# Token scalings as one GpSimd product per tile, and a norm-factor chain of two GpSimd operations

## The chip, the cores and the metric

The kernel runs on one core of a Trainium2 chip. The metric is the device time of one execution in microseconds (us). TensorE does the matrix products, VectorE, ScalarE and GpSimd the elementwise work; in the profile they are PE (with PEld for its weight loads), DVE, ACT and POOL. Each engine takes its instructions in the order in which they were written, and engines wait for each other through semaphores (`wait_ge`, `then_inc`).

## What is computed

One transformer layer of width 256 on 2048 tokens (32 sequences of 64): attention with quantized projections, then a mixture of experts (the second part is not touched). Cut to what matters here:

```
def _div_clamp_fp8(x, scale):
    y = jnp.clip(x / scale, -448, 448)
    return _fp8_roundtrip(y.astype(bfloat16).astype(float32))
ln_out = _ln(hidden_states, ln_w, ln_b)
q  = _ln(linear(_div_clamp_fp8(ln_out, q_in_scale),  wq),  qln_w,  qln_b)
k  = _ln(linear(_div_clamp_fp8(ln_out, k_in_scale),  wk),  kln_w,  kln_b)
v  =     linear(_div_clamp_fp8(ln_out, v_in_scale),  wv)
qx = _ln(linear(_div_clamp_fp8(ln_out, qx_in_scale), wqx), qxln_w, qxln_b)
kx = _ln(cond @ w_kx, kxln_w, kxln_b);  vx = cond @ w_vx
out = linear(_div_clamp_fp8(concat(attend(q, k, v), attend(qx, kx, vx)), smooth), wproj)
```

So every token tile is divided by four different vectors (K, Q, V and QX), clipped and rounded to fp8 values: four quantized copies. `_ln` over a head of 128 needs, for each token and head, a factor (variance + 1e-5)^(-1/2).

## The kernel before

The tokens are NT = 16 tiles of 128. Attention over them is 64 slots, four to a tile (r = 0 to 3): r is the half of the heads, with self attention in r = 0, 1 and cross attention in r = 2, 3. In a slot N the engines work on several slots at once, as a software pipeline: `run_slots` goes through a written list of steps for each engine, each with a number "ahead", and calls the step for slot N + ahead. Nothing is planned at run time: the lists are the order of the instructions.

In a slot PE does four projections into `b_pj` (L346) for slot N+3, three groups of transposes of normalised heads (L362, `b_tr<-ident,nrm`) for N+2, the scores (L374), the transposes of the probabilities (L393), the products with the values (L403) and the output projection (L446). ACT squares each projection (L458, `sq`), copies it (L468, `raw`), and evicts transposes (L485, with the weight and bias of the head norm from `col`). DVE sums the squares (L526, `ssq`), and multiplies `raw` by the norm factor (L537, `nrm<-raw,rstd`) before PE transposes it; it also does the softmax (L546 to L569), `cat` (L578) and `catq` (L587, L593), the quantizing of attention's output.

Two steps are touched by the change.

The norm factors (`pool_rstd`, L693 to L704) are on POOL: four operations from `ssq` to `rstd`, var = ssq * unit2, vareps = var + eps, root = vareps^(-1/2), rstd = root * unit. They run twice in a slot: once on 4 factors (the K heads, for `nrm` 0 of that slot) and once on 8 (the Q heads, for `nrm` 1 and 2 at the start of the next).

The token scalings belong to the steps with "ahead" PREP = 7: a tile's tokens are prepared seven slots early, in parts 0 to 3. In part 0 DVE normalises (L671, `n<-x_sb`), PE transposes (L628), ACT evicts with the layer norm's weight and bias (L637, `lnT`). In each of the four parts ACT then divides `lnT` by one of the four scales (L647, `y<-lnT,rin`, two instructions, one for each half of the width), and DVE clips (L678, `xq<-y`) and rounds (L682, `xq<-xq`) that copy. On POOL stands besides, once in a tile, a small layer norm for the second half of the kernel (`pool_rows`, L716 to L720, `zero<-x_sb`: names are those of the memory, its result is called n3).

Of the kernel before, what the change touches and what calls it, by code (L numbers as in the profile page):

```python
# [5 lines left out]
F32 = mybir.dt.float32  # L6
F16 = mybir.dt.float16
BF16 = mybir.dt.bfloat16
# [57 lines left out]
def build(nc, x, ctxT, cols, w_all, wprojT,  # L66
# [4 lines left out]
    with ExitStack() as top:  # L71
# [6 lines left out]
        def sem(name):  # L78
# [51 lines left out]
                 "small_done st_done t_done ssum_done stot_done sstep sinv_done wsq4_done csum_done ctot_done wscale_done n2_done tr_done ctx_step "  # L130
                 "ctxh_done xh_done lnt_done raw_done proj_done norm_done tev_done sub_done sc_done pn_done "
                 "ptev_done pt_done cev_done pv_done catq_done x1_done po_done ssq_done sq_done exp_done rs_done "
                 "mx_done sum_done rc_done clip_done pool_var pool_ve pool_pw ve3 rs3 rw_in zero_set xbuf_zero "
# [24 lines left out]
        with ExitStack() as ph:  # L158
# [5 lines left out]
            y16 = sb("y16", [P, 2, KT, P], BF16, ph)  # L164
# [22 lines left out]
            var = sb("var", [P, 2, NN, HC], F32, ph)  # L187
            vareps = sb("vareps", [P, 2, NN, HC], F32, ph)
            root = sb("root", [P, 2, NN, HC], F32, ph)
# [78 lines left out]

            def wide(ap, n):
                return ap.unsqueeze(2).to_broadcast([P, ap.shape[1], n])  # L270
# [50 lines left out]
            def pe_project(c):  # L321
                def step(pe, N):
# [12 lines left out]
                    if r == 0 and c in (0, 1, 3):  # L335
                        pe.wait_ge(s["xq_done"], 4 * i + (1, 2, 0, 3)[c])
                    if r == 2 and c == 1:
                        pe.wait_ge(s["xq_done"], 4 * i + 4)
                    if i == 0:
                        pe.wait_ge(s["wlo_done"], unit_number(r, c, KT - 1) + 1)  # L340
# [135 lines left out]
            def act_tev(c):  # L476
                def step(act, N):
# [6 lines left out]
                    at = C_HLN + 2 * ((HLN_K if c == 0 else HLN_Q) + kind)  # L484
                    act.activation(flat(dst), b_tr[:, :], ACT.Identity, scale=col[:, at:at + 1],  # L485
                                   bias=col[:, at + 1:at + 2]).then_inc(s["tev_done"], 1)
# [144 lines left out]
            def act_token(act, t, part):  # L631
# [3 lines left out]
                after(act, "y_done", 4 * t)  # L635
# [5 lines left out]
            def act_token_scaled(act, t, part):  # L641
# [3 lines left out]
                after(act, "q16_done", 4 * t + part - 1)  # L645
                for k in range(KT):
                    last = act.activation(y16[:, part % 2, k, :], lnT[:, k, :], ACT.Copy, scale=rin[:, j, k:k + 1])  # L647
                last.then_inc(s["y_done"], 1)

# [24 lines left out]
            def dve_quantize(dve, t, part):  # L674
                M = 4 * t + part
                dst = xq_all[:, ring(t), :, PARTS[part], :]
                dve.wait_ge(s["y_done"], M + 1)
                dve.tensor_scalar(dst, y16[:, part % 2, :, :], FP8_MAX * DOWN, -FP8_MAX * DOWN, ALU.min, ALU.max)\  # L678
# [5 lines left out]
            def pool_rstd(q):  # L684
                def step(pool, N):
# [7 lines left out]
                    pool.tensor_tensor(var[:, r % 2, c, :], ssq[:, r % 2, c, :],  # L693
                                       unit2[:, j:j + 1].unsqueeze(2).to_broadcast(shape), ALU.mult)\
                        .then_inc(s["pool_var"], 1)
                    pool.wait_ge(s["pool_var"], e)
# [5 lines left out]
                    pool.wait_ge(s["pool_pw"], e)  # L702
# [89 lines left out]
            def attention_scalar(act, tail):  # L792
# [28 lines left out]
                def context_high(n):  # L821
# [27 lines left out]
                    (PREP, act_token_scaled, "tokens"),  # L849
# [6 lines left out]
                    (-3, "tokens"): lambda: (act_token_scaled(act, 0, 3), act_token(act, 1, 0), act_token_scaled(act, 1, 0)),  # L856
# [1052 lines left out]
```

## Time and profile before

| | before |
|---|---|
| median of 3 runs | 955.73 us (955.66 to 956.96) |
| the profiled execution, its own time | 956.31 us |
| its span, first to last instruction | 954.5 us |
| PE busy | 916.9 us, 96% |
| DVE busy | 793.8 us, 83% |
| ACT busy | 735.6 us, 77% |
| POOL busy | 454.5 us, 48% |

The span has three parts: up to about 110 us the weights and the context are prepared beside the first slots; up to about 635 us the slots run in a pattern that repeats with each tile; then comes the mixture of experts. A matmul's duration in a row includes its way through the array, so that the rows of consecutive matmuls overlap; what a matmul costs is the distance to the start of the next one, and a wait of PE shows as a start that comes later than that. A row with several instructions (x4) begins with the first of them.

### The profile page before, as it was taken

To read this page: it belongs to the slowest core of one execution; us is meant where nothing else is said; L and a number is where in the kernel's file an instruction comes from. 1 tells how busy PE (TensorE), PEld (TensorE's weight loads), DVE (VectorE), ACT (ScalarE), POOL (GpSimd) and SP (SyncE) were. 2 spreads that over 40 slices of the span, in tenths; PEclk is the share of its full clock that TensorE was granted. 3 is DMA by queue.
4 is the path that set the end of the run, shared out by engine and by line. 5 is a ranking of instruction groups with operands and counts; after the bars stand their busy time and mean duration, and the time that the engine had idled before them with its cause. 6 is when DMAs were issued, how large, how long until landed. Compare 5 with 4: busy or idle time off the path is not lost.

```text
span 954.5 us, 23599 instructions
## 1 busy us (share of the span) xinstructions
PE 916.9 (96%) x8264; PEld 621.1 (65%) x8264; DVE 793.8 (83%) x1720; ACT 735.6 (77%) x1370; POOL 454.5 (48%) x673
## 2 busy tenths in 40 slices
PE   5688999999999999999999999999999999999997
PEld 3365666766767676766767667666655566666665
DVE  6889999999999999999999999987998744444443
ACT  5998899899899899899999999864656545555554
POOL 5335656465565555555555555531056513333333
PEclk9989999999999999999999999999999999999999
DMA  9933201001001001001100100213558713333323
GB/s 215 333 90 70 64 24 51 30 30 44 29 30 46 29 29 46 29 30 31 44 30 24 52 29 24 102 44 117 178 157 262 249 48 54 51 74 51 46 32 37
DMA packets 36754, 70.48 MB, mean 74 GB/s; under 512 B 3616, under 2 KB 24736, under 8 KB 36512
## 3 DMA queue, kind: packets, MB, share of 16 engines
q1 hardware_dynamic: 27184, 54.39, 17.5%
q0 software_dynamic: 9456, 14.59, 9.1%
q8 instruction: 70, 1.15, 0.5%
q14 instruction: 44, 0.36, 0.1%
HBM read 55.52 MB, written 18.68 MB: 78 GB/s over the span
## 4 chain that ended last, share of the span: by engine, by line
PE 64%; DVE 21%; issue 7%; ACT 5%; POOL 1%; DMA 1%; DVEq 0%; POOLq 0%; ACTq 0%
PE b_pj L346 17%; PE b_tr L362 7%; PE b_pj L1339 5%; PE b_o L403 5%; PE b_o L1374 5%; PE b_sc L374 4%; PE b_acc L446 4%; PE b_o L1466 3%; PE b_tr L1339 3%; DVE ssq L526 3%; PE b_sc L1339 3%; DVE nrm L537 3%; PE b_pj L1419 2%; DVE cat L578 2%; PE b_pt L1363 2%
## 5 line engine op out<-in xcount | busy, mean ns | idle before, releaser
L700 POOL TENSOR_TENSOR root<-vareps,neghalf 128x4 f32<-128x4 f32 (+1 forms) x128 | 173.8, 1358 | 10.0
L693 POOL TENSOR_TENSOR var<-ssq,unit 128x4 f32<-128x4 f32 (+1 forms) x128 | 54.3, 424 | 235.1 <-DVE ssq L526 235.1
L346 PE MATMUL b_pj<-w_hi,xq 128*128 128x512 f16 x384 | 148.9, 388 | 1.1 <-DVE xq L682 0.8
L346 PE MATMUL b_pj<-w_lo,xq 128*128 128x512 f16 x384 | 148.3, 386 | 0.0
L526 DVE TENSOR_REDUCE ssq<-sq 128x4 f32<-128x512 f32 x192 | 130.3, 679 | 3.3 <-ACT sq L458 2.1
L537 DVE TENSOR_TENSOR nrm<-raw,rstd 128x512 f32<-128x512 f32 x192 | 128.8, 671 | 4.2 <-POOL rstd L704 3.5
L362 PE MATMUL b_tr<-ident,nrm 128*128 128x128 f32 x768 | 120.5, 280 | 11.6 <-DVE nrm L537 7.0
L458 ACT ACTIVATE sq<-b_pj 128x512 f32<-128x512 f32 x192 | 114.2, 595 | 18.2 <-PE b_pj L346 14.7
L1315 POOL DMA_INDIRECT out<-xn x39 | 60.6, 1553 | 136.2 <-ACT xn L1545 110.5
L362 PEld LDWEIGHTS b_tr<-ident,nrm 128*128 128x128 f32 x768 | 87.7, 141 | 48.3 <-DVE nrm L537 18.1
L468 ACT ACTIVATE raw<-b_pj 128x512 f32<-128x512 f32 x192 | 116.0, 604 | 0.0
L485 ACT ACTIVATE qT<-b_tr,col 128x512 f32<-128x512 f32 x128 | 99.7, 779 | 1.4 <-PE b_tr L362 1.4
L578 DVE TENSOR_TENSOR cat<-b_o,rsm 128x512 bf16<-128x512 f32 x128 | 81.9, 682 | 1.4 <-PE b_o L403 1.4
L374 PEld LDWEIGHTS b_sc<-kT,qT 128*64 128x64 f32 x2048 | 64.9, 138 | 18.6 <-issue 14.6
L374 PE MATMUL b_sc<-kT,qT 128*64 128x64 f32 x2048 | 73.8, 225 | 0.7 <-ACT qT L485 0.7
L403 PE MATMUL b_o<-probT,v 64*128 64x128 f32 x1024 | 74.4, 285 | 0.0
L403 PEld LDWEIGHTS b_o<-probT,v 64*128 64x128 f32 x1024 | 62.1, 188 | 11.5 <-issue 11.5
L446 PE MATMUL b_acc<-wproj,catq 128*128 128x256 f16 x512 | 66.4, 273 | 0.0
L346 PEld LDWEIGHTS b_pj<-w_hi,xq 128*128 128x128 f16 x384 | 37.8, 99 | 33.1 <-issue 1.4
L492 ACT ACTIVATE prob<-prob 128x512 f32<-128x512 f32 x64 | 40.7, 636 | 22.4 <-DVE prob L553 22.1
L485 ACT ACTIVATE kT<-b_tr,col 128x512 f32<-128x512 f32 x64 | 49.5, 774 | 9.6 <-PE b_tr L362 8.4
L346 PEld LDWEIGHTS b_pj<-w_lo,xq 128*128 128x128 f16 x384 | 38.1, 99 | 25.2 <-issue 1.9
(327 smaller groups left out, 2271.7 us busy)
## 6 DMA issues: line engine op xcount, KB each, us to landing
nst<-in_ffw SPq DMA_DIRECT2D x40, 512.0 KB, 3.3
wload<-in_ffw SPq DMA_DIRECT2D x20, 512.0 KB, 4.5
xbuf<-zero SPq DMA_DIRECT2D x13, 387.0 KB, 9.6
xn<-xbuf SPq DMA_DIRECT2D x9, 516.0 KB, 3.7
x_sb<-in_x SPq DMA_DIRECT2D x4, 512.0 KB, 14.1
wproj<-in_ctxT SPq DMA_DIRECT2D x1, 2048.0 KB, 10.9
xhl<-in_w_all SPq DMA_DIRECT2D x4, 512.0 KB, 18.2
wproj<-in_wprojT POOLq DMA_DIRECT2D x4, 512.0 KB, 5.0
```

Source lines behind the costliest of these rows:

```text
L346: last = pe.matmul(o, x, w[kind][:, k, at:at + BANK], start=(k == 0 and n_ == 0), stop=(k == KT - 1 and n_ == len(terms) - 1))
L362: last = pe.transpose(o, nrm[:, c, hd * P:(hd + 1) * P], ident[:, :])
L374: last = pe.matmul(b_sc[rows, (g * 2 + b) * S:(g * 2 + b + 1) * S], qT[:, r % 2, g * 2 + b, rows], kT[:, r % 2, g, b * S:(b + 1) * S], sta ...
L403: last = pe.matmul(b_o[b][:, g * P:(g + 1) * P], v[b * S:(b + 1) * S, N % 4, g, :], probT[b * S:(b + 1) * S, r % 2, g, :], start=True, sto ...
L446: last = pe.matmul(out_sum(i), catq[:, r % 2, hd, :], wproj[:, r * n + hd, :], start=(r == 0 and hd == 0 and i != 1), stop=(r == 3 and hd ...
L458: act.activation(sq[:, m % 2, :], b_pj[c % 2][:, :], ACT.Square).then_inc(s["sq_done"], 1)
L468: act.activation(raw[:, r % 2, c, :], bk, ACT.Copy).then_inc(s["raw_done"], 1)
L485: act.activation(flat(dst), b_tr[:, :], ACT.Identity, scale=col[:, at:at + 1], bias=col[:, at + 1:at + 2]).then_inc(s["tev_done"], 1)
L526: dve.tensor_reduce(ssq[:, r % 2, c, :], sq[:, m % 2, :].rearrange("p (a b) -> p a b", b=D), axis=AX.X, op=ALU.add).then_inc(s["ssq_done"], 1)
L537: dve.tensor_tensor(nrm[:, c, :].rearrange("p (a b) -> p a b", b=D), raw[:, r % 2, c, :].rearrange("p (a b) -> p a b", b=D), wide(rstd[:, ...
L700: pool.tensor_tensor(root[:, r % 2, c, :], vareps[:, r % 2, c, :], neghalf[:, 0:1].unsqueeze(2).to_broadcast(shape), ALU.pow).then_inc(s[" ...
L1339: last = pe.matmul(o[:, :], xx[n][:, k * P:(k + 1) * P], w[:, bass.ds(e, 1), at:at + F].rearrange("p a b -> p (a b)"), start=(k == 0 and m ...
```

## The change

The diff, cut to its core (waits, lists and names that follow from it are left out):

```diff
-            y16 = sb("y16", [P, 2, KT, P], BF16, ph)
+            y16 = sb("y16", [P, KT, 4, P], BF16, ph)
+            hw = sb("hw", [P, 4], F32, ph)
...
+            def scaled(t):
+                return 4 * t if t < 2 else t + 6
...
-                    if r == 0 and c in (0, 1, 3):
+                    if i < 2 and r == 0 and c in (0, 1, 3):
...
+                    if i >= 2 and r == 0 and c == 0:
+                        pe.wait_ge(s["xq_done"], scaled(i) + 1)
...
+                    if c == 0 and N in (0, SLOTS.index((0, 2))):
+                        act.wait_ge(s["hw_done"], 1 + kind)
-                    act.activation(flat(dst), b_tr[:, :], ACT.Identity, scale=col[:, at:at + 1],
+                    act.activation(flat(dst), b_tr[:, :], ACT.Identity, scale=hw[:, j:j + 1],
...
+            def pool_token_scaled(pool, t, part):
+                if part != 1:
+                    return
+                pool.wait_ge(s["lnt_done"], KT * t + KT)
+                pool.wait_ge(s["q16_done"], scaled(t))
+                pool.tensor_tensor(y16[:, :, :, :], lnT[:, :, :].unsqueeze(2).to_broadcast([P, KT, 4, P]),
+                                   rin[:, :, :].rearrange("p j k -> p k j").unsqueeze(3).to_broadcast([P, KT, 4, P]),
+                                   ALU.mult).then_inc(s["y_done"], 1)
...
             def dve_quantize(dve, t, part):
-                M = 4 * t + part
-                dst = xq_all[:, ring(t), :, PARTS[part], :]
+                if t >= 2 and part != 2:
+                    return
+                j = slice(0, 4) if t >= 2 else PARTS[part]
+                M = scaled(t) if t >= 2 else 4 * t + part
+                dst = xq_all[:, ring(t), :, j, :]
...
-                    pool.tensor_tensor(var[:, r % 2, c, :], ssq[:, r % 2, c, :],
-                                       unit2[:, j:j + 1].unsqueeze(2).to_broadcast(shape), ALU.mult)\
...
-                    pool.tensor_tensor(vareps[:, r % 2, c, :], var[:, r % 2, c, :],
-                                       epsc[:, 0:1].unsqueeze(2).to_broadcast(shape), ALU.add).then_inc(s["pool_ve"], 1)
+                    pool.tensor_scalar(vareps[:, r % 2, c, :], ssq[:, r % 2, c, :], unit2[:, j:j + 1], EPS,
+                                       ALU.mult, ALU.add).then_inc(s["pool_ve"], 1)
...
-                    pool.tensor_tensor(root[:, r % 2, c, :], vareps[:, r % 2, c, :],
-                                       neghalf[:, 0:1].unsqueeze(2).to_broadcast(shape), ALU.pow).then_inc(s["pool_pw"], 1)
...
-                    pool.tensor_tensor(rstd[:, r % 2, c, :], root[:, r % 2, c, :],
-                                       unit[:, j:j + 1].unsqueeze(2).to_broadcast(shape), ALU.mult)\
+                    pool.tensor_tensor(rstd[:, r % 2, c, :], vareps[:, r % 2, c, :],
+                                       neghalf[:, 0:1].unsqueeze(2).to_broadcast(shape), ALU.pow)\
...
-                    (PREP, act_token_scaled, "tokens"),
...
+                dve.tensor_tensor(hw[:, 0:3], col[:, C_HLN:C_HLN + 6:2], unit[:, 0:3], ALU.mult).then_inc(s["hw_done"], 1)
...
+                    dve.tensor_tensor(hw[:, 3:4], col[:, C_HLN + 6:C_HLN + 7], unit[:, 4:5], ALU.mult).then_inc(s["hw_done"], 1)
...
-                run_slots(pool, [(3, pool_rstd(0)), (3, pool_rstd(1)), (ROWS, pool_rows)],
+                run_slots(pool, [(3, pool_rstd(0)), (3, pool_rstd(1)), (ROWS, pool_rows), (PREP, pool_token_scaled)],
```

For the tiles from 2 on, the four scaled copies are written by one POOL product of 1024 elements in each partition (`y<-lnT,rin`), in part 1, instead of by eight ACT instructions; DVE clips and rounds all four at once, in part 2, instead of one in each part. Tiles 0 and 1 keep the old way. The four POOL operations of a norm factor become two; the factor `unit` is multiplied once, at the start, into the head norm's weight (`hw`), with which ACT evicts the transposes anyway.

The order on POOL in the slot of part 1, before (the chain of the 8 factors, then those of the next slot):

```order
L693 TENSOR_TENSOR var<-ssq,unit 128x8
L697 TENSOR_TENSOR vareps<-var,epsc 128x8
L700 TENSOR_TENSOR root<-vareps,neghalf 128x8
L704 TENSOR_TENSOR rstd<-root,unit 128x8
L693 TENSOR_TENSOR var<-ssq,unit 128x4
L697 TENSOR_TENSOR vareps<-var,epsc 128x4
L700 TENSOR_TENSOR root<-vareps,neghalf 128x4
L704 TENSOR_TENSOR rstd<-root,unit 128x4
```

The same place after the change (POOL):

```order
L712 TENSOR_SCALAR vareps<-ssq,unit 128x8
L716 TENSOR_TENSOR rstd<-vareps,neghalf 128x8
L662 TENSOR_TENSOR y<-lnT,rin 128x1024
L712 TENSOR_SCALAR vareps<-ssq,unit 128x4
L716 TENSOR_TENSOR rstd<-vareps,neghalf 128x4
```

The product stands between the factors of the Q heads of one slot and those of the K heads of the next.

The end of the slot of part 2 and the start of the next on DVE, before:

```order
L587 TENSOR_SCALAR catq<-cat 128x1024
L593 TENSOR_SCALAR catq<-catq 128x1024
L678 TENSOR_SCALAR xq<-y 128x2x128
L682 TENSOR_SCALAR xq<-xq 128x2x128
L546 TENSOR_REDUCE mx<-b_sc 128x8
L537 TENSOR_TENSOR nrm<-raw,rstd 128x512
```

And after (DVE, the same place):

```order
L594 TENSOR_SCALAR catq<-cat 128x1024
L600 TENSOR_SCALAR catq<-catq 128x1024
L697 TENSOR_SCALAR xq<-y 128x1024
L701 TENSOR_SCALAR xq<-xq 128x1024
L553 TENSOR_REDUCE mx<-b_sc 128x8
L544 TENSOR_TENSOR nrm<-raw,rstd 128x512
```

The pair stays in the list in this slot and is four times as large; in the slots of parts 0, 1 and 3 nothing stands in its place.

## Rows read from the trace of the kernel before

**Rows 1.** Busy time (and instructions) by engine in one tile's stretch, then clock, DMA:

```profile
294.70:331.30 36.60, 36.52 (x373) 25.60 (x372) 35.39 (x73) 33.43 (x65) 20.82 (x36) 1.00 0.10 34
```

**Rows 2.** Timeline of PE: start, duration, line, operands, count:

```profile
305.81 0.38 PE L346 MATMUL b_pj<-w_lo,xq 128*128 128x512 f16 x1
306.27 0.66 PE L362 MATMUL b_tr<-ident,nrm 128*128 128x128 f32 x4
...
324.73 0.38 PE L346 MATMUL b_pj<-w_lo,xq 128*128 128x512 f16 x1
324.95 0.60 PE L362 MATMUL b_tr<-ident,nrm 128*128 128x128 f32 x4
```

**Rows 3.** Waits of PE, 75 to 112 us: total, times, longest:

```profile
PE b_tr L362 <- DVE nrm L537: 3.9, 5, 1.3
```

**Rows 4.** Waits of PE's weight loads, 330 to 367 us:

```profile
PEld b_tr L362 <- DVE nrm L537: 0.6, 1, 0.6
```

**Rows 5.** Waits of PE, 587 to 625 us:

```profile
PE b_tr L362 <- DVE nrm L537: 1.0, 1, 1.0
```

**Rows 6.** Chain of waits through one tile: start, length, what:

```profile
330.84 0.69 ACT y L647 x2
...
342.84 0.66 PE b_tr L362 x4
```

**Rows 7.** Timeline of DVE in the same tile, with idle time before and its releaser:

```profile
301.78 0.64 DVE L537 TENSOR_TENSOR nrm<-raw,rstd 128x512 f32<-128x512 f32 x1
302.34 0.69 DVE L569 TENSOR_TENSOR prob<-prob,rc 128x512 f32<-128x512 f32 x1
...
306.73 0.69 DVE L537 TENSOR_TENSOR nrm<-raw,rstd 128x512 f32<-128x512 f32 x1
...
312.18 0.42 DVE L587 TENSOR_SCALAR catq<-cat 128x1024 f16<-128x1024 bf16 x1
312.63 0.43 DVE L593 TENSOR_SCALAR catq<-catq 128x1024 uint16<-128x1024 uint16 x1
312.97 0.22 DVE L678 TENSOR_SCALAR xq<-y 128x256 f16<-128x256 bf16 x1
313.23 0.23 DVE L682 TENSOR_SCALAR xq<-xq 128x256 uint16<-128x256 uint16 x1
313.37 0.42 DVE L618 SCALAR_TENSOR_TENSOR xr<-zero,xr 128x256 f16<-128x256 f32 x1
...
314.40 0.69 DVE L537 TENSOR_TENSOR nrm<-raw,rstd 128x512 f32<-128x512 f32 x1
...
319.89 0.64 DVE L537 TENSOR_TENSOR nrm<-raw,rstd 128x512 f32<-128x512 f32 x1
...
323.28 0.69 DVE L537 TENSOR_TENSOR nrm<-raw,rstd 128x512 f32<-128x512 f32 x1 [0.23 <-POOL rstd L704]
...
331.55 0.23 DVE L678 TENSOR_SCALAR xq<-y 128x256 f16<-128x256 bf16 x1 [0.52 <-ACT y L647]
```

**Rows 8.** Timeline of POOL in the same tile:

```profile
301.84 0.65 POOL L693 TENSOR_TENSOR var<-ssq,unit 128x8 f32<-128x8 f32 x1 [1.13 <-DVE ssq L526]
302.56 0.52 POOL L697 TENSOR_TENSOR vareps<-var,epsc 128x8 f32<-128x8 f32 x1
303.17 1.69 POOL L700 TENSOR_TENSOR root<-vareps,neghalf 128x8 f32<-128x8 f32 x1
304.94 0.20 POOL L704 TENSOR_TENSOR rstd<-root,unit 128x8 f32<-128x8 f32 x1
...
306.11 1.23 POOL L720 TENSOR_SCALAR zero<-x_sb,mv,rs 128x256 f32<-128x256 f32 x1
...
308.65 1.03 POOL L700 TENSOR_TENSOR root<-vareps,neghalf 128x4 f32<-128x4 f32 x1
```

**Rows 9.** Other POOL operations, grouped by line and shape: busy, mean ns:

```profile
L1107 POOL MEMSET zero<- 128x1548 f16 x1 | 1.4, 1407 | 0.0
L1091 POOL TENSOR_SCALAR_AFFINE_SELECT ident<-ident 128x128 f32<-128x128 f32 x1 | 0.3, 291 | 0.3 <-POOL ident L1089 0.3
```

More of the change, by code:

```diff
@@ L334, in step @@
                         terms = ((j, w_hi), (j, w_lo))
-                    if r == 0 and c in (0, 1, 3):
+                    if i < 2 and r == 0 and c in (0, 1, 3):
                         pe.wait_ge(s["xq_done"], 4 * i + (1, 2, 0, 3)[c])
-                    if r == 2 and c == 1:
+                    if i < 2 and r == 2 and c == 1:
                         pe.wait_ge(s["xq_done"], 4 * i + 4)
+                    if i >= 2 and r == 0 and c == 0:
+                        pe.wait_ge(s["xq_done"], scaled(i) + 1)
                     if i == 0:
@@ L483, in step @@
                     dst = kT[:, r % 2, :, :] if c == 0 else qT[:, r % 2, (c - 1) * 4:c * 4, :]
-                    at = C_HLN + 2 * ((HLN_K if c == 0 else HLN_Q) + kind)
-                    act.activation(flat(dst), b_tr[:, :], ACT.Identity, scale=col[:, at:at + 1],
-                                   bias=col[:, at + 1:at + 2]).then_inc(s["tev_done"], 1)
+                    if c == 0 and N in (0, SLOTS.index((0, 2))):
+                        act.wait_ge(s["hw_done"], 1 + kind)
+                    j = (HLN_K if c == 0 else HLN_Q) + kind
+                    at = C_HLN + 2 * j + 1
+                    act.activation(flat(dst), b_tr[:, :], ACT.Identity, scale=hw[:, j:j + 1],
+                                   bias=col[:, at:at + 1]).then_inc(s["tev_done"], 1)
                 return step
@@ L634, in act_token @@
                 act.wait_ge(s["tr_done"], t + 1)
-                after(act, "y_done", 4 * t)
+                after(act, "y_done", scaled(t))
                 for k in range(KT):
@@ L644, in act_token_scaled @@
                     act.wait_ge(s["lnt_done"], KT * t + KT)
-                after(act, "q16_done", 4 * t + part - 1)
+                after(act, "q16_done", 4 * t + part - 3)
                 for k in range(KT):
-                    last = act.activation(y16[:, part % 2, k, :], lnT[:, k, :], ACT.Copy, scale=rin[:, j, k:k + 1])
+                    last = act.activation(y16[:, k, j, :], lnT[:, k, :], ACT.Copy, scale=rin[:, j, k:k + 1])
                 last.then_inc(s["y_done"], 1)
+            def pool_token_scaled(pool, t, part):
[6 more added lines that the diff above has]
+                                   ALU.mult).then_inc(s["y_done"], 1)
             def dve_scale_chain(dve, n, at, sums):
@@ L674, in dve_quantize @@
             def dve_quantize(dve, t, part):
-                M = 4 * t + part
-                dst = xq_all[:, ring(t), :, PARTS[part], :]
+                if t >= 2 and part != 2:
[3 more added lines that the diff above has]
+                dst = xq_all[:, ring(t), :, j, :]
                 dve.wait_ge(s["y_done"], M + 1)
-                dve.tensor_scalar(dst, y16[:, part % 2, :, :], FP8_MAX * DOWN, -FP8_MAX * DOWN, ALU.min, ALU.max)\
+                dve.tensor_scalar(dst, y16[:, :, j, :], FP8_MAX * DOWN, -FP8_MAX * DOWN, ALU.min, ALU.max)\
                     .then_inc(s["q16_done"], 1)
@@ L860, in attention_scalar @@
                     (-2, "raw 3"): lambda: high(2, 4),
-                    (-2, "token"): lambda: (high(2, 5), squares(0)),
-                    (-2, "tokens"): lambda: (squares(1), high(3, 2), squares(2)),
+                    (-2, "token"): lambda: (high(2, 5), squares(0), squares(1), high(3, 2), squares(2)),
                     (-2, "rows"): lambda: (high(3, 3), squares(3)),
@@ L868, in attention_scalar @@
                     (-1, "raw 2"): lambda: act_token_scaled(act, 1, 3),
-                    (-1, "tokens"): lambda: (high(2, 0), high(2, 1)),
+                    (-1, "token"): lambda: (high(2, 0), high(2, 1)),
                     (0, "weight squares"): lambda: high(2, 6),
@@ L1586, in shared @@
                     return run
-                tail = {(FIRST - 3, "tokens"): shared(0), (FIRST - 2, "raw 1"): shared(1), (FIRST - 1, "raw 3"): units_known}
+                tail = {(FIRST - 3, "token"): shared(0), (FIRST - 2, "raw 1"): shared(1), (FIRST - 1, "raw 3"): units_known}
                 for n in range(JOIN):
@@ L1592, in _ @@
                 for n in range(2, 6):
-                    tail[FIRST - 2 + n, "tokens"] = shared(n)
+                    tail[FIRST - 2 + n, "token"] = shared(n)
                 attention_scalar(act, tail)
```

11 lines of the change are left out of this document (3 added, 8 removed).

## The prediction

> **What bounds the kernel now.** I read the busy times by stretch first, then PE's timeline and its waits, then the chain of waits, then DVE and POOL beside each other in one tile. In a tile of the repeating part PE is busy 36.52 of 36.60 us, DVE 35.39, ACT 33.43, POOL 20.82, with the clock at its higher level of 2.4 GHz (granted 1.00) [rows 1]. A busy PE may still hide waits, so the starts decide. Where nothing is late, the transposes of `nrm` start 0.22 us after the start of the last projection matmul (324.73 to 324.95); at 305.81 the same pair is 0.46 us apart [rows 2]. PE thus waits 0.24 to 0.25 us, for `nrm` from DVE. I went along all starts of PE: this wait comes once in a tile, from 196 to 562 us in eleven tiles, and once as 0.46 us in the tile before. The list of waits has it as the single wait for `nrm` in a tile (0.6 us on the weight loads, which run ahead of the matmuls) [rows 4]. So from 110 to 600 us PE is the bound, and all that the other engines can give back is about 3.2 us. The rest lies at the ends: 3.9 us of waits for `nrm` in five places between 75 and 112 us, where DVE also prepares the context [rows 3], and 1.0 us near 599 us [rows 5].
>
> The chain shows why `nrm` is late: it leaves PE for ACT's scaling `y` of part 3 at 330.84, goes on over DVE, and comes back to PE's transposes at 342.84 [rows 6]. 342.84 less 306.27 [rows 2] is the period of a tile, 36.57 us. DVE had stood idle for 0.52 us for that `y` [rows 7].
>
> **The change, part by part.**
>
> ACT's eight scalings in a tile go, 0.69 us for a pair [rows 6]. ACT is not the bound; what counts is that DVE no longer waits for them: 0.52 us in part 3.
>
> On DVE, a clip and a rounding of one copy take 313.37 - 312.97 = 0.40 us from start to start; the same two on 1024 elements, the pair that quantizes attention, take 312.97 - 312.18 = 0.79 us [rows 7]. The change removes 0.40 in parts 0, 1 and 3 and adds 0.39 in part 2: 0.81 us less in a tile, 1.33 with the wait. In part 2's slot `nrm` ends at 323.28 + 0.69 = 323.97, and PE takes it at 324.95 [rows 2, 7]: 0.98 us of cover for the added 0.39. In the slots of parts 3 and 0, which lead to the late `nrm`, DVE gains 0.92 and 0.40 us, and 0.25 is wanted.
>
> On POOL, the 8 factors take from 301.84 to 305.14. `var` is 0.65 us long beside an `nrm` on DVE and ends 0.07 after it; `vareps` is 0.52 beside `prob`, and ends 0.05 after that [rows 7, 8]; without such a neighbour an operation of this size takes the 0.20 of `rstd`. POOL thus stands still while DVE reads two SBUF tensors. In the new chain the first operation still waits for `nrm`, and the power then waits for `prob` in place of `vareps`, so only `rstd` and its gap go and a little of the power's delay: about 0.35 us of 3.3. The factors of the K heads gain two small operations with their gaps, 0.55 us. `nrm` was 0.23 us late by POOL in one slot of a tile [rows 7]; that place moves with DVE, and nothing replaces it.
>
> The product is new: 1024 elements from two f32 operands. The trace has no POOL operation like it, so bounds: a MEMSET writes 1548 elements in 1.41 us, which makes 0.93 us for 1024; the AFFINE_SELECT reads and writes 128 in 0.29, 2.3 us for 1024 [rows 9]; n3 takes 1.23 for 256, 4.9 us for 1024 [rows 8]. I take 2.4 us, by the AFFINE_SELECT, the row nearest in kind, and keep 0.9 and 4.9 for the range. It starts right after the 8 factors, at about 314.05 (`nrm` at 314.40 marks their end today, less 0.35) [rows 7]. Two `nrm` lie in its way, which hold POOL for 0.6 us each: it ends at 314.05 + 2.4 + 1.2 = 317.65. Behind it the K factors need 0.20 + 0.07 + 1.03 = 1.30 [rows 8] and are there at 318.95; the `nrm` that takes them starts at 319.89, or 0.4 earlier now [rows 7]. So it is hidden, with 0.5 us to spare. The quantizing that waits for it stands nine microseconds later.
>
> The Trainium skill (GPSIMD Engine Reference, 3.1 Elementwise) gives a two-input `tensor_tensor` of 2048 elements 4497 ns on GpSimd. An estimate from that page is 2.25 us for the product; by it the sum stays the same, and no row here shows it.
>
> `hw` adds two tiny DVE operations at the start, 0.1 us on the way; the eviction reads another scale, at the same price.
>
> The sum: twelve repeated waits, 11 x 0.25 + 0.46 = 3.2 us. Of the 3.9 us early on, DVE has 0.40 less in parts 0 and 1 of tile 2 and a shorter POOL chain, against 0.39 more in part 2: I take 1.0. Of the 1.0 near 599 us, where part 3 of the last tile stands a slot ahead, 0.3. After 600 us 0.2 from the shorter chain. Less 0.1 for `hw`: 4.6 us. The profiled execution's 956.31 becomes 951.7; it was 0.58 above the median of the runs, 955.73, which becomes 951.1.
>
> **Rivals.**
>
> DVE held by the product (22%). `nrm` and the product read SBUF at the same time. Suppose that POOL, once it has begun, keeps DVE's two-tensor operations off until its end. `nrm` 1 goes first, the product begins behind it, and `nrm` 2, due 0.6 us later, is held for 2.4 - 0.6 = 1.8 us. DVE carries this into part 2's slot with 0.39 more and 0.40 less, against the cover of 0.98: PE waits 0.8 us in each of 14 tiles, 11.2 us less the 4.6: 962.3. Should `nrm` 1 be held as well, nothing covers it: up to 2.4 x 14 = 34 us. Against it: n3 runs from 306.11 to 307.34, and the `nrm` that starts within it, at 306.73, lasts 0.69 us as always [rows 7, 8]; likewise at all its sixteen places. For it: n3 is short and may have read all before. The Trainium skill (SBUF — State Buffer, SBUF: two separate sides) states exactly this rival: whichever starts first has the shared pair for its whole instruction, and the other is fully blocked. For `var` behind `nrm` the trace agrees; for `nrm` within n3 it doesn't.
>
> The product is long (8%). It decides above 319.49 - 1.30 - 1.2 - 314.05 = 2.9 us. At n3's 4.9, the K factors come 2.0 us late, DVE stands for it and 0.39 more follows: against the cover of 0.98, PE waits about 1.0 us in 14 tiles, less 4.6: 965.
>
> The gain doesn't arrive (13%). PE has no slack of its own, and `nrm` may be late behind something else, for instance ACT's squares, which set when `ssq` can start. Then only the early part gives something: 955.0.
>
> **How the numbers follow.** Forecast 57%: 951.1, its own range 948.5 (all waits of rows 3 and 5 gone as well) to 953.5. Of the rest, 30% is slower and 13% mostly no change. What a measurement of this kernel can tell from no change is 0.2%, 1.9 us. Faster: the forecast's 57% and a little of the third rival, 0.59; same 0.13; slower 0.28. The range is 948.5 to 962.5: it takes in the first rival's lower price and the third, and leaves out the long product and a `nrm` 1 that is held.
>
> **What would show it.** PE's start of the transposes 0.22 us behind the projection in every slot, and a period of 36.3 us for a tile. POOL's product at 2.3 to 3.6 us, the K factors done before `nrm` asks. DVE without a wait for `y`, and in part 1's slot `nrm` 1 and 2 still 1.2 us apart. Wrong it is when these two move apart by more than a microsecond, when a wait of `nrm` for `rstd` grows in the slot of part 2, or when the period stays 36.57.

## The result, and the profile after

The changed kernel takes 964.6 us (963.49 to 967.39, 4 runs), against 955.72 (955.66 to 956.96, 4 runs) for the kernel before on the same chip: 1.0095 times as long, with an interval of 1.0082 to 1.0107. It is slower by 8.9 us; forecast was 951.1, and the range ended at 962.5. One run of e10 (968.86 us) and one of e11 (1060.55 us) fell into a slower state of the chip, and all medians below are of the other, fast runs. The profiled run is the longest of the four, 967.39 us with a span of 965.6.

The first two rows of the page of the changed kernel show the load where it was meant to be: ACT and POOL have less to do.

```profile
span 965.6 us, 23136 instructions
...
PE 917.1 (95%) x8264; PEld 621.5 (64%) x8264; DVE 807.9 (84%) x1638; ACT 704.2 (73%) x1258; POOL 446.2 (46%) x431
```

ACT has lost 31 us and PE has the same work. But DVE, which was to be relieved of 0.81 us in every tile, is busy 14 us longer. The groups by line name the one that grew: `nrm` on DVE, and next to it POOL's new product (busy time and mean ns of one, then idle time before).

```profile
L544 DVE TENSOR_TENSOR nrm<-raw,rstd 128x512 f32<-128x512 f32 x192 | 150.5, 784 | 3.7 <-POOL rstd L716 0.9 <-issue 0.2
...
L366 PE MATMUL b_tr<-ident,nrm 128*128 128x128 f32 x768 | 120.8, 280 | 18.2 <-DVE nrm L544 14.4 <-ACT kT L492 1.9 <-ACT qT L492 1.8
...
L662 POOL TENSOR_TENSOR y<-lnT,rin 128x1024 bf16<-128x1024 f32 x14 | 26.6, 1897 | 0.0
```

The same 192 `nrm` were 128.8 us busy before, 671 ns each: 21.7 us have come in. A mean of 784 hides that nearly all of them are unchanged. The busy times of one tile give the place to look at: a stretch of one period, to hold against [rows 1].

```profile
300.53:337.53 37.00, 36.50 (x372) 25.58 (x370) 36.38 (x69) 31.04 (x58) 20.58 (x20) 1.00 0.10 33
```

A tile now takes 37.00 us where it took 36.58 (the distance from an `nrm` to the same one ten tiles later, divided by ten, in each of the two traces). PE's busy time hardly moved and its clock is the same granted 1.00; DVE is at 36.38 of 37.00. The timeline of DVE around the product, with start and duration (the counterpart of [rows 7]), shows why:

```profile
316.23 0.69 DVE L553 TENSOR_REDUCE mx<-b_sc 128x8 f32<-128x512 f32 x1
317.04 2.38 DVE L544 TENSOR_TENSOR nrm<-raw,rstd 128x512 f32<-128x512 f32 x1
319.35 0.68 DVE L560 TENSOR_TENSOR prob<-b_sc,mx 128x512 f32<-128x512 f32 x1
319.95 0.68 DVE L544 TENSOR_TENSOR nrm<-raw,rstd 128x512 f32<-128x512 f32 x1
```

And the timeline of POOL at the same place (that of [rows 8]):

```profile
314.00 1.23 POOL L712 TENSOR_SCALAR vareps<-ssq,unit 128x8 f32<-128x8 f32 x1 [1.60 <-DVE ssq L533]
315.32 1.69 POOL L716 TENSOR_TENSOR rstd<-vareps,neghalf 128x8 f32<-128x8 f32 x1
316.98 1.90 POOL L662 TENSOR_TENSOR y<-lnT,rin 128x1024 bf16<-128x1024 f32 x1
321.32 0.27 POOL L712 TENSOR_SCALAR vareps<-ssq,unit 128x4 f32<-128x4 f32 x1 [2.44 <-DVE ssq L533]
```

Both things wait for the power at L716. When it ends, POOL goes on in its own list and starts the product at 316.98; DVE is released by the same end, and starts `nrm` 1 at 317.04, 0.06 us later. That `nrm` lasts 2.38 us instead of 0.68. It ends at 319.42, which is 0.54 after the product's end at 318.88: about the length of an undisturbed `nrm`. So it did nothing while the product ran. PE's timeline has the price:

```profile
318.60 0.38 PE L350 MATMUL b_pj<-w_lo,xq 128*128 128x512 f16 x1
319.48 0.66 PE L366 MATMUL b_tr<-ident,nrm 128*128 128x128 f32 x4 [0.50 <-DVE nrm L544]
...
321.82 0.38 PE L350 MATMUL b_pj<-w_lo,xq 128*128 128x512 f16 x1
322.03 0.60 PE L366 MATMUL b_tr<-ident,nrm 128*128 128x128 f32 x4
...
346.56 0.38 PE L350 MATMUL b_pj<-w_lo,xq 128*128 128x512 f16 x1
346.78 0.60 PE L366 MATMUL b_tr<-ident,nrm 128*128 128x128 f32 x4
```

PE could have started at 318.60 + 0.22 = 318.82 and started at 319.48, 0.66 late. `nrm` 1 undisturbed would have ended at 317.72, with 1.10 us to spare for PE; it was held for 2.38 - 0.68 = 1.70; 1.70 - 1.10 is 0.60, and 0.06 is the step from the end of the one to the start of the other. At the two other places PE runs 0.21 and 0.22 us behind the projection, and the one at 346.78 answers, counted along PE's instructions, to the late one of the kernel before (306.27 in [rows 2], 342.84 a tile later): the wait of 0.24 that the change was to remove has gone.

One product lies in the early part, beside the preparation of the context, where it hits another DVE operation with two SBUF tensors. From the timelines of POOL and then of DVE:

```profile
91.36 1.89 POOL L662 TENSOR_TENSOR y<-lnT,rin 128x1024 bf16<-128x1024 f32 x1
```

```profile
91.33 3.00 DVE L1012 SCALAR_TENSOR_TENSOR ctxl<-wproj,nsc,ctxh 128x1024 f16<-128x1024 f32 x1
...
103.26 1.28 DVE L1012 SCALAR_TENSOR_TENSOR ctxl<-wproj,nsc,ctxh 128x1024 f16<-128x1024 f32 x1
```

Here DVE's record even begins 0.03 us before the product's, and it is still the one that is stretched, by 1.72 us. PE's transposes behind it waited 1.19 us in place of 0.24.

### The profile page after: what moved, and what is told of

Its sections match the earlier page's. It is cut to its first block, busy times and chain, and to the rows that moved or that the text cites. A ratio compares the mean times of both kernels' runs of the same rounds, so it can differ in the third digit from the quotient of the medians.

```text
span 965.6 us, 23136 instructions
## 1 busy us (share of the span) xinstructions
PE 917.1 (95%) x8264; PEld 621.5 (64%) x8264; DVE 807.9 (84%) x1638; ACT 704.2 (73%) x1258; POOL 446.2 (46%) x431
## 4 chain that ended last, share of the span: by engine, by line
PE 31%; POOL 28%; issue 24%; DVE 12%; ACT 4%; another core or an unknown queue 0%; POOLq 0%; DVEq 0%; ACTq 0%
POOL rstd L716 14%; POOL vareps L712 8%; PE b_o L1386 5%; PE b_pj L1351 5%; PE b_pj L350 3%; PE b_tr L1351 3%; PE b_sc L1351 3%; PE b_o L1478 2%; POOL y L662 2%; PE b_pt L1375 2%; POOL zero L732 2%; PE b_pj L1431 2%; DVE a L1776 1%; PE b_sc L1431 1%; ACT w_hi L813 1%
## 5 line engine op out<-in xcount | busy, mean ns | idle before, releaser
L712 POOL TENSOR_SCALAR vareps<-ssq,unit 128x4 f32<-128x4 f32 (+1 forms) x128 | 93.2, 728 | 266.8 <-DVE ssq L533 266.6
L716 POOL TENSOR_TENSOR rstd<-vareps,neghalf 128x4 f32<-128x4 f32 (+1 forms) x128 | 173.0, 1351 | 10.7
L544 DVE TENSOR_TENSOR nrm<-raw,rstd 128x512 f32<-128x512 f32 x192 | 150.5, 784 | 3.7 <-POOL rstd L716 0.9
L492 ACT ACTIVATE qT<-b_tr,col,hw 128x512 f32<-128x512 f32 x128 | 100.6, 786 | 1.8 <-PE b_tr L366 1.8
L492 ACT ACTIVATE kT<-b_tr,col,hw 128x512 f32<-128x512 f32 x64 | 50.1, 782 | 25.6 <-PE b_tr L366 25.5
```

Of the source, the lines that this page charges most:

```text
L492: act.activation(flat(dst), b_tr[:, :], ACT.Identity, scale=hw[:, j:j + 1], bias=col[:, at:at + 1]).then_inc(s["tev_done"], 1)
L544: dve.tensor_tensor(nrm[:, c, :].rearrange("p (a b) -> p a b", b=D), raw[:, r % 2, c, :].rearrange("p (a b) -> p a b", b=D), wide(rstd[:, ...
L712: pool.tensor_scalar(vareps[:, r % 2, c, :], ssq[:, r % 2, c, :], unit2[:, j:j + 1], EPS, ALU.mult, ALU.add).then_inc(s["pool_ve"], 1)
L716: pool.tensor_tensor(rstd[:, r % 2, c, :], vareps[:, r % 2, c, :], neghalf[:, 0:1].unsqueeze(2).to_broadcast(shape), ALU.pow)\
```

## The experiments

Changes are given against the changed kernel where nothing else is said. "Period" is the time of a tile in the repeating part, measured as above; "at the end of the slots" is how much later (+) than in the trace of the kernel before the instructions around 640 us start. That column is no finer than about 1 us: at 60 us, ahead of every product, the traces of the changed kernel and of e1, e2, e5, e6, e7, e8, e10 and e11 hold the same instructions and already lie between 0.9 us early and 0.2 us late, and the stretches before 58 us in which PE's clock was granted at 0.50 (1.2 GHz) differ among them. The kernel before was run again beside every group of them, with medians of 956.2 to 956.3 us.

| | median us | ratio to before, interval | period | at the end of the slots |
|---|---|---|---|---|
| changed kernel | 964.6 | 1.0095 (1.0082 to 1.0107) | 37.00 | +7.1 |
| e1_wait: product waits for `nrm` 2 | 951.68 | 0.996 (0.9946 to 0.9973) | 36.29 | -4.9 |
| e8_ahead: product first in the list | 951.96 | 0.9958 (0.9942 to 0.9973) | 36.29 | -5.1 |
| e2_no_product | 953.89 | 0.9976 (0.9966 to 0.9986) | 36.29 | -3.8 |
| e4_tokens_only | 967.53 | 1.0119 (1.0104 to 1.0135) | 37.33 | +10.3 |
| e3_chain_only | 956.73 | 1.0003 (0.9994 to 1.0012) | 36.58 | +0.5 |
| e7_twice | 973.79 | 1.0183 (1.016 to 1.0206) | 37.66 | +17.3 |
| e5_split4 | 953.44 | 0.997 (0.9958 to 0.9982) | 36.29 | -3.6 |
| e6_one_input | 952.41 | 0.997 (0.9946 to 0.9994) | 36.29 | -5.2 |
| e9_wait_old_chain | 952.8 | 0.9967 (0.9956 to 0.9978) | 36.28 | -3.9 |
| e10_eight_scalars | 953.03 | 0.9973 (0.9964 to 0.9983) | 36.28 | -4.3 |
| e11_after_first | 954.61 | 0.999 (0.9974 to 1.0006) | 36.28 | -3.1 |

**e1_wait: the product at a place without a neighbour.** Nothing is removed; the product only waits until both `nrm` of the slot are done.

```diff
                 pool.wait_ge(s["q16_done"], scaled(t))
+                pool.wait_ge(s["norm_done"], NN * (4 * t - 3) + NN)
                 pool.tensor_tensor(y16[:, :, :, :], ...
```

> The changed kernel with one wait more: the product waits until nrm 2 of the next slot is done, and so runs beside the sum of squares and cat. Theory (the product keeps DVE's two-tensor nrm from starting for its whole 1.9 us): no nrm over 0.7 us, no wait of PE for nrm in the tile, period 36.3 to 36.4 us instead of 37.0, in all 950 to 953 us. Rival (the loss comes from the other edits: the shorter POOL chain's slower first operation of 1.23 us, or the pair of 1024 elements on DVE): the nrm shortens but the period stays near 37.0 and the time within 960 to 965.

Measured: 951.68 us, the period 36.29. POOL's timeline, then DVE's:

```profile
309.10 1.69 POOL L717 TENSOR_TENSOR rstd<-vareps,neghalf 128x8 f32<-128x8 f32 x1
312.88 1.90 POOL L663 TENSOR_TENSOR y<-lnT,rin 128x1024 bf16<-128x1024 f32 x1 [2.10 <-DVE nrm L544]
314.76 0.27 POOL L713 TENSOR_SCALAR vareps<-ssq,unit 128x4 f32<-128x4 f32 x1
```

```profile
310.82 0.69 DVE L544 TENSOR_TENSOR nrm<-raw,rstd 128x512 f32<-128x512 f32 x1
312.03 0.68 DVE L544 TENSOR_TENSOR nrm<-raw,rstd 128x512 f32<-128x512 f32 x1
316.64 0.64 DVE L544 TENSOR_TENSOR nrm<-raw,rstd 128x512 f32<-128x512 f32 x1
```

The same product with the same length, 2.1 us later, and every `nrm` has its old duration. The factors behind it are ready at 316.13, before the `nrm` that takes them, at 316.64. One line is worth 12.9 us against the changed kernel (964.6 - 951.68), and the result is 0.4% faster than the kernel before, with an interval that leaves out 1. None of DVE's operations beside the product (`ssq`, `sm`, `cat`) reads two large SBUF tensors. The place of the product was the whole loss.

**e8_ahead: the same, with another order on POOL.** The product comes first in POOL's list for the slot and waits for the `nrm` of the slot before.

```diff
+                pool.wait_ge(s["norm_done"], NN * (4 * t - 4) + NN)
...
-                run_slots(pool, [(3, pool_rstd(0)), (3, pool_rstd(1)), (ROWS, pool_rows), (PREP, pool_token_scaled)],
+                run_slots(pool, [(PREP, pool_token_scaled), (3, pool_rstd(0)), (3, pool_rstd(1)), (ROWS, pool_rows)],
```

> The changed kernel with the product first in POOL's list of the slot of part 1 (one slot half earlier than with the wait in the next slot), behind a wait for nrm 2 of the same slot. Theory: no nrm is held, the same gain as with the other wait, 951 to 952.5 us; the ctxl operations at 77 to 104 us lie elsewhere, so the start may differ by 1 us. Rival (POOL is late with the factors of the K heads): nrm 0 waits for rstd in this slot, over 953 us.

Measured: 951.96, with the period of e1. It is not a property of one gap: it is enough that none of DVE's `nrm` is due in the 1.9 us.

**e2_no_product: the product nearly taken out.** One column of 128 is left of it, except in tile 2; the tokens of the later tiles are thus mostly not scaled.

```diff
-                pool.tensor_tensor(y16[:, :, :, :], lnT[:, :, :]...to_broadcast([P, KT, 4, P]),
+                m = P if t == 2 else 1
+                pool.tensor_tensor(y16[:, :, :, 0:m], lnT[:, :, 0:m]...to_broadcast([P, KT, 4, m]),
```

> The changed kernel with the product left out for the tiles from 3 on (one column of 128 is written, so the quantized tokens are wrong there). It is the most that the change can give without the product's cost. Theory: 950 to 953 us, the same as with the wait. Rival (other edits lose): over 958 us.

Measured: 953.89, 0.9 us above the range that I had expected, and far from the rival's 958. The period is 36.29, to the hundredth that of e1 with the whole product. Well placed, the product costs nothing in a tile. The 1.1 us by which it ends later than e1 stem from tile 2, whose product is whole and unmoved here: its instructions around 119 us are 0.4 late, those of e1 0.7 early.

**e4_tokens_only and e3_chain_only: the two halves of the change apart.** e4 is the kernel before with the product and the pair of four scales, and the old chain of four operations; e3 is the kernel before with the new chain and `hw`, and ACT's scalings as they were.

```diff
 e4, against the changed kernel
-                    pool.tensor_scalar(vareps..., ssq..., unit2[:, j:j + 1], EPS, ALU.mult, ALU.add)
+                    pool.tensor_tensor(var..., ssq..., unit2..., ALU.mult)
+                    pool.tensor_tensor(vareps..., var..., epsc..., ALU.add)
...
-                    pool.tensor_tensor(rstd..., vareps..., neghalf..., ALU.pow)
+                    pool.tensor_tensor(root..., vareps..., neghalf..., ALU.pow)
+                    pool.tensor_tensor(rstd..., root..., unit..., ALU.mult)
 e3, against the changed kernel
-                pool.tensor_tensor(y16[:, :, :, :], ...
+                    last = act.activation(y16[:, part % 2, k, :], lnT[:, k, :], ACT.Copy, scale=rin[:, j, k:k + 1])
```

> The kernel before with the product and the merged pair, and the old chain of four POOL operations. Theory: nrm 1 is held as in the changed kernel, DVE is a little later by POOL's longer chain: 963 to 967 us. Rival (the chain is what loses): within 2 us of the kernel before.

> The kernel before with the chain of two POOL operations and the head norm's weight scaled at the start; the tokens as before. Theory: the chain of the 8 factors is 0.3 us shorter, but nrm is late by DVE and not by POOL in the slot that holds PE up, so little changes in the tile: 954 to 955.5 us. Rival (the chain costs): 957 us or more.

Measured: the tokens alone are slower still (967.53), the chain alone makes no difference (956.73; the interval of the ratio takes in 1). They lie 0.5 and 1.2 us above their expected ranges. Of e4, POOL and then DVE:

```profile
318.05 1.91 POOL L661 TENSOR_TENSOR y<-lnT,rin 128x1024 bf16<-128x1024 f32 x1
```

```profile
318.13 2.37 DVE L543 TENSOR_TENSOR nrm<-raw,rstd 128x512 f32<-128x512 f32 x1 [0.41 <-POOL rstd L722]
```

The hold is the same with the old chain. It costs more here, since `nrm` also waits 0.41 us for POOL: PE starts 0.99 late, and the period is 0.33 longer than with both halves. In one tile of e4 the order is the other one: `nrm` 1 starts at 169.49 us, 0.13 ahead of the product. There `nrm` 1 has its usual 0.69 us, the product takes 2.33, `nrm` 2 takes 1.80, and PE doesn't wait for either. So the loss does not come from the chain; and a chain that is 0.3 us shorter is worth nothing by itself, since ACT's `y`, not POOL, ends DVE's wait in that kernel [rows 7].

**e7_twice: twice the suspected cost.** The product is made twice, the first time into memory that nobody reads.

```diff
+                for dst in (y16b, y16):
-                pool.tensor_tensor(y16[:, :, :, :], ...
+                    last = pool.tensor_tensor(dst[:, :, :, :], ...
```

> The changed kernel with the product issued twice, first into a scratch tile and then as before. Theory (the hold is a price on DVE, lasting as long as the product): DVE is held for 1.9 us more, either in nrm 1 or in nrm 2. PE had 0.66 us of wait for the first 1.9 us; the cover is used up, so nearly all of the second comes through: 1.5 to 1.9 us in 14 tiles, 985 to 992 us. Rival (POOL itself is what is late): the factors of the K heads come later and nrm 0 waits for rstd, nrm 1 stays at 2.4 us; under 975 us.

Measured: 973.79, slower by 9.2 than the changed kernel, but well short of the expectation. POOL's timeline, then DVE's:

```profile
321.92 1.90 POOL L664 TENSOR_TENSOR y16b<-lnT,rin 128x1024 bf16<-128x1024 f32 x1
323.77 2.35 POOL L664 TENSOR_TENSOR y<-lnT,rin 128x1024 bf16<-128x1024 f32 x1
```

```profile
321.98 2.38 DVE L545 TENSOR_TENSOR nrm<-raw,rstd 128x512 f32<-128x512 f32 x1
324.89 1.79 DVE L545 TENSOR_TENSOR nrm<-raw,rstd 128x512 f32<-128x512 f32 x1
```

I had let `nrm` 1 be held through both products. It isn't: between the two it gets in, and now the second product is the one that stands, 2.35 - 1.90 = 0.45 us; it then holds `nrm` 2 for 1.79 - 0.68 = 1.11. Per tile PE waits 0.95 and 0.30 us, in place of 0.66. The rival's bound of 975 us holds as well, but not its reason: no `nrm` waits for `rstd` behind the two products. So the hold goes by instruction and in both directions. That pointed to the next experiment.

**e5_split4: the same work in four instructions.**

```diff
+                for j in range(4):
+                    last = pool.tensor_tensor(y16[:, :, j, :], lnT[:, :, :],
+                                              rin[:, j, :].unsqueeze(2).to_broadcast([P, KT, P]), ALU.mult)
```

> The changed kernel with the product as four POOL instructions of 256 elements, one for each scale, at the same place. Theory (the port is held for one instruction and no longer): nrm 1 is held once, by about 0.5 us (a quarter of 1.9), then DVE and POOL take turns; PE's wait of 0.66 us in the tile goes; 951 to 955 us. Rival (a row of POOL instructions keeps DVE out like one): a nrm of 2.4 us or more as now, 963 to 967 us.

Measured: 953.44, at the place where one instruction gave 964.6, without any added wait. POOL (four instructions in a row), then DVE:

```profile
312.05 3.22 POOL L663 TENSOR_TENSOR y<-lnT,rin 128x256 bf16<-128x256 f32 x4
```

```profile
312.12 1.09 DVE L544 TENSOR_TENSOR nrm<-raw,rstd 128x512 f32<-128x512 f32 x1
...
313.73 1.07 DVE L544 TENSOR_TENSOR nrm<-raw,rstd 128x512 f32<-128x512 f32 x1
```

Each `nrm` is held for some 0.4 us, under the 1.10 of cover, and PE doesn't wait for it in the repeating tiles. POOL pays for it: 3.22 us for the four in place of 1.90. They take turns with DVE: the first and third take 0.61 us, the second and fourth, which `nrm` holds in its turn, 1.06.

**e6_one_input: the same writes, one tensor read.** All four copies with the first scale, by an operation whose factor is one number for each partition; the copies thus have the wrong scale, and the eight factors of the second operand are not read.

```diff
-                pool.tensor_tensor(y16[:, :, :, :], lnT..., rin...to_broadcast([P, KT, 4, P]),
+                pool.tensor_scalar(y16[:, :, :, :], lnT..., rin[:, 0, 0:1], None, ALU.mult)
```

> The changed kernel with the product as one POOL TENSOR_SCALAR of 1024 elements: it reads one tensor and multiplies all by a single scale (so the quantized tokens of the tiles from 2 on are wrong there). Theory A (any POOL instruction that reads SBUF holds DVE's two-tensor operations): nrm 1 is as long as this instruction plus 0.5 us, time by its length, 957 to 970 us. Theory B (only a two-tensor instruction of POOL does, which would explain why n3 did not): no nrm over 0.7 us, 951 to 955 us.

POOL, then DVE:

```profile
310.40 3.38 POOL L662 TENSOR_SCALAR y<-lnT,rin 128x1024 bf16<-128x1024 f32 x1
```

```profile
310.45 0.69 DVE L544 TENSOR_TENSOR nrm<-raw,rstd 128x512 f32<-128x512 f32 x1
311.66 0.92 DVE L544 TENSOR_TENSOR nrm<-raw,rstd 128x512 f32<-128x512 f32 x1
```

The operation is 1.8 times as long as the product, started 0.05 us ahead of `nrm` 1 as the product does, and didn't hold it at all; it held `nrm` 2 for 0.24 us. `nrm` 2's 0.92 is 0.22 more than my Theory B allowed. So it isn't the length of the POOL instruction that decides. The kind differs, and with it the second tensor that is read; the run changes both at once. The row of n3 on which I had judged is a TENSOR_SCALAR as well [rows 8].

**e10_eight_scalars: a version of all four scales in that kind.**

```diff
+                for j in range(4):
+                    for k in range(KT):
+                        last = pool.tensor_scalar(y16[:, k, j, :], lnT[:, k, :], rin[:, j, k:k + 1], None, ALU.mult)
```

> The changed kernel with the product as eight POOL TENSOR_SCALARs of 128 elements, each of one tensor and its own scale, at the product's place; it computes the same. In the run with one TENSOR_SCALAR of 1024 elements nrm 1, which began 0.05 us behind it, was not held, and nrm 2 by 0.24 us. Theory (a one-tensor instruction holds DVE for a small part of its time): no nrm over 1.0 us; about 0.6 us each, 4.5 to 5 us for the eight, so the factors of the K heads may come 0 to 1 us late: 951 to 954 us. Rival (each short instruction holds nrm like a part of the product): nrm 1 and 2 over 1.05 us each as with four products, 953 to 955 us.

```profile
311.31 5.39 POOL L664 TENSOR_SCALAR y<-lnT,rin 128x128 bf16<-128x128 f32 x8
```

Measured: 953.03, period 36.28. The eight take 5.39 us, hold `nrm` by 0.1 at most, and are themselves held: the first, begun 0.05 us ahead of `nrm` 1, takes 1.14 us and the third 0.80, where the others take 0.60. They make the later factors late (a later `nrm` waits 0.83 us for POOL), which PE doesn't see. It is as good as e5 and no better than e1.

**e9_wait_old_chain: e4 with the wait of e1.**

> The product behind a wait for nrm 2 of the next slot, with the old chain of four POOL operations (only the tokens are changed). If the gain of the version with the wait comes from DVE's shorter work for the tokens alone, this gives the same within 0.5 us in the repeating part: 951.5 to 952.5 us. If the shorter chain is needed once DVE is earlier (nrm 1 would then wait for rstd), the period lies between 36.28 and 36.57 us: 953 to 955 us.

Measured: 952.8, 0.3 above the first range, but with the period of the first case, 36.28, although `nrm` waits 0.41, 0.23 and 0.34 us for POOL in each tile. The cure thus doesn't need the new chain. Against e1 it is 1.1 us slower by the medians and 0.9 by the traces around 640 us; the intervals of the two ratios overlap, and 0.3 of the 0.9 is there at 60 us, so a gain by the chain is not shown.

**e11_after_first: the order that my first rival had assumed.** The product waits for `nrm` 1 only.

```diff
+                pool.wait_ge(s["norm_done"], NN * (4 * t - 3) + NN - 1)
```

> The changed kernel with a wait of the product for nrm 1 instead of nrm 2: the order that the prediction took for its first rival. Theory (first come, first served, until the end of the instruction): nrm 1 takes 0.69 us, nrm 2 is held and takes 0.68 + 1.9 - 0.6 = about 1.8 to 2.0 us. DVE loses 1.2 us in the tile instead of 1.7; PE needs nrm 2 only 2 us after nrm 1, so less of it comes through: 951.5 to 957 us. Rival (the hold costs the same wherever it falls): 961 us or more.

POOL, DVE and PE:

```profile
313.48 1.90 POOL L663 TENSOR_TENSOR y<-lnT,rin 128x1024 bf16<-128x1024 f32 x1 [0.90 <-DVE nrm L544]
```

```profile
312.61 0.69 DVE L544 TENSOR_TENSOR nrm<-raw,rstd 128x512 f32<-128x512 f32 x1
313.82 2.10 DVE L544 TENSOR_TENSOR nrm<-raw,rstd 128x512 f32<-128x512 f32 x1
```

```profile
316.52 0.38 PE L350 MATMUL b_pj<-w_lo,xq 128*128 128x512 f16 x1
316.73 0.60 PE L366 MATMUL b_tr<-ident,nrm 128*128 128x128 f32 x4
```

`nrm` 2 is held 1.42 us, and PE doesn't wait for it: 316.73 is 0.21 behind the projection, and the period stays 36.28. In this order the hold costs nothing in a tile. Its median is 2.9 us above e1, of which the traces show 1.8 ahead of 640 us, in the early tiles.

## Why the prediction was wrong

**The step that failed** is in the working of the product: "Two `nrm` lie in its way, which hold POOL for 0.6 us each". The holding was there, its direction was wrong. The product does not come behind `nrm` 1: POOL, which takes the next instruction of its own list, started it 0.06 us before DVE, which had to be released, started `nrm` 1. I had computed 314.05 for the start of the product and had 314.40 for that of `nrm` before the change, which is the same 314.05 once the chain's 0.35 is taken off: a tie by my own numbers, since both start at the end of the same POOL operation. I then let `nrm` go first, without a reason, and so put DVE's loss at nothing where 1.70 us were measured. And a two-tensor product that is ahead keeps the `nrm` out to its end. e1, which takes only the coincidence away, moves the time from 964.6 to 951.68. The prediction's own sign of being wrong is there too: `nrm` 1 and 2 start 2.91 us apart, not 1.2.

**The reading that misled.** Against the rival I had put n3, which starts before an `nrm` and doesn't hold it [rows 8]. e6 shows that this says nothing of a product: a TENSOR_SCALAR of 3.38 us holds the first `nrm` by nothing and the next by 0.24, a TENSOR_TENSOR of 1.90 holds it by 1.70. (That `nrm` lies within n3 at 14 of its 16 places, not at all sixteen.) The evidence that the two engines share something was on the same page: `var` and `vareps` on POOL are stretched by DVE's two-tensor operations. Of the reverse case the trace before had only harmless examples, and they were TENSOR_TENSORs. POOL, then DVE, of the kernel before:

```profile
305.45 0.55 POOL L718 TENSOR_TENSOR rs<-ve,neghalf 128x1 f32<-128x1 f32 x1
312.39 1.70 POOL L700 TENSOR_TENSOR root<-vareps,neghalf 128x8 f32<-128x8 f32 x1
```

```profile
305.53 0.68 DVE L537 TENSOR_TENSOR nrm<-raw,rstd 128x512 f32<-128x512 f32 x1
```

Here an `nrm` that starts 0.08 us into `rs` lasts its usual 0.68, and `xr`, which reads two SBUF tensors and starts at 313.37 [rows 7], is not held 0.98 us into a `root` of 1.70 (nor 0.57 into the new chain's power of 1.69). These POOL operations read 1 and 8 elements in each partition, the product 1024. So the kind alone doesn't decide either: a row that clears or accuses the product would have had to be a TENSOR_TENSOR with many elements, and the trace before had none.

The Trainium skill (SBUF — State Buffer, SBUF: two separate sides) states the rule in both directions: of a GpSimd operation and a DVE operation with two SBUF inputs, the first to start has the shared port pair for its whole instruction. For the product the runs agree (2.38, 2.37 and 2.10 us for `nrm`; 3.00 for `ctxl`, though there DVE's record is the earlier by 0.03). For POOL's TENSOR_SCALAR they don't, as e6 and e10 show, nor do they for the short TENSOR_TENSORs above.

**The first rival** (22%) had the mechanism and missed its terms. The order was the other one, `nrm` 1 held and not `nrm` 2. The product took 1.90 us, not 2.4. For a held `nrm` 1 I wrote that "nothing covers it" and put it at up to 34 us; there are 1.10 us of cover, and 0.66 of the 1.70 came through. For a held `nrm` 2 I had 0.8 us of wait in a tile; e11 shows none. That its 962.3 lies 2.3 from the measured time is thus mostly luck. (The lower end of the range was also mis-added: with all waits of [rows 3] and [rows 5] gone it is 947.5, not 948.5. Nothing hangs on it.)

**The sum of the changed kernel**, by its own trace: the repeated 0.25 us waits are gone and 0.66 is new; a tile is 0.42 longer. Against e1 a tile is 0.71 longer, 13 tiles make 9.2. At 119 us, behind tile 2's product, the changed kernel is 2.1 behind e1 (1.4 late against 0.7 early). That is 11.3 of the 12.0 us that lie between the two traces at 640 us. But only 1.5 of the 2.1 come behind the start of that product, where it holds `ctxl`. At 76 us the changed kernel was 0.5 ahead of e1, and at 84 us 0.6 behind, before any product: PE had stood idle for 1.59 us, and then ran with a granted clock of 0.50 (1.2 GHz) up to 83 us, where e1's trace has 1.00. The stretch from 80 us in the trace of the changed kernel (the 0.50 near the end is the clock):

```profile
80.00:81.00 1.00, 1.00 (x5) 0.60 (x4) 1.00 (x3) 0.51 (x3) 0.00 (x0) 0.50 0.00 0
```

No other trace here has the lower clock between 58 us and the last microseconds, so this 1.1 us belongs to the profiled run and not to the change.

**Second rival**, the long product: refuted. It took 1894 to 1901 ns in all 14 places, nearer to the AFFINE_SELECT's 2.3 than to the ends 0.9 and 4.9, and below the 2.9 from which it would matter. e10 shows that even 5.39 us of POOL work at this place costs nothing in a tile: the later `nrm` is 0.83 late by POOL, and PE doesn't see it.

**Third rival**, that the gain doesn't arrive: refuted by e1, where all of it does.

**What was right**, once the product is out of the way: 951.68 us against the forecast 951.1; period 36.29 against 36.3; at the end of the slots 4.9 us early, for a sum of 4.6 (3.3 of it between 160 and 600 us, for 3.2 in the sum; 1.3 from 60 to 160 us, for 1.0; nothing at or behind 600 us, for 0.5); no wait for `y`, and the merged pair, 0.80 us from start to start, hidden. The new chain's gain was about as I had it, for the reason that I gave: its first operation still stands beside `nrm` and `prob` and lasts 1.23 us (0.27 for the four factors, where nothing stands beside it), and from the start of the chain to that of the power it is 315.32 - 314.00 = 1.32 us, before 1.33 [rows 8]. Only `rstd` has gone. e3 and e9 show that this is worth nothing in a tile; ahead of the repeating tiles no gain by it is shown (e3 ends the slots 0.5 us later than the kernel before).

**What stays open.** In its profiled run the changed kernel loses 2.1 us more around 751 us, in the second half of the kernel, where this row stands on DVE (its releaser is not seen), and another 1.7 behind ACT's last instruction:

```profile
751.87 1.41 DVE L1830 SCALAR_TENSOR_TENSOR x_sb<-b_o,us,x_sb 128x512 f32<-128x512 f32 x2 [4.62 <-remote]
```

The change doesn't touch that part, and in e1's trace it runs as before (the same row stands there behind 2.17 us of idle time, for PE). The spans of the other runs of the changed kernel are 963.1, 961.8 and 962.6 us, against 965.6 for this one, so part of it belongs to the one run; I have no trace of another. Nor is it settled why a TENSOR_SCALAR on POOL leaves DVE alone, or from how many elements on a TENSOR_TENSOR holds it: between the 8 of `root`, which doesn't, and the 256 of e5, which do, no run has a value.

## What to carry to other kernels

Before work is moved to POOL, list which DVE operations with two SBUF tensors will run at the same time, and who starts first, to a tenth of a microsecond. Where two instructions waited for the same end here, the engine that had finished its own work was the first, by 0.05 to 0.08 us. A long two-tensor instruction on POOL belongs in a gap between such operations (in e1 a wait on the last of them was enough), or is cut into pieces shorter than the cover of whatever it can hold (e5). And a row that is to speak for a new operation must be of the same kind and size, not only of the same engine.

## What the runs showed of the hardware

- POOL TENSOR_TENSOR, f32 by f32 to bf16: 1.90 us for 1024 elements; of 256 elements 0.61, or 1.06 when an `nrm` holds it (3.22 for four). A TENSOR_SCALAR with a factor for each partition takes 3.38 us for 1024 and 5.39 for eight of 128 (0.60 each where nothing holds it): the operation with less to read is the slower one.
- A POOL product of two tensors that started 0.06 to 0.09 us before a two-tensor DVE operation held it in the changed kernel, e4, e5 and e7, and so it did with `ctxl` although DVE's record began 0.03 earlier. With DVE 0.13 us ahead (one tile of e4) it was the product that was held. With 0.34 us between them (e11) the product held the `nrm` behind it for the whole rest of its length.
- POOL TENSOR_TENSORs of 1 and 8 elements, 0.55 and 1.70 us long, held no DVE operation of two SBUF tensors that started within them.
- A TENSOR_SCALAR on POOL gives way: in e10 one that was 0.05 us ahead of an `nrm` took 1.14 us in place of 0.60; in e4 n3, begun at the same instant as an `nrm`, took 1.79 us in place of 1.23, and the `nrm` its usual 0.69. POOL, then DVE, of e4:

```profile
310.45 1.79 POOL L738 TENSOR_SCALAR zero<-x_sb,mv,rs 128x256 f32<-128x256 f32 x1
```

```profile
310.45 0.69 DVE L543 TENSOR_TENSOR nrm<-raw,rstd 128x512 f32<-128x512 f32 x1
```
